# Seven block products in place of eight for the second graph layer, and aggregation columns divided at 250 and 750

## The chip, the cores and the metric

The kernel runs on one core of a Trainium2 chip. The metric is the device time of one execution in microseconds (us); lower is better. An engine is named by what it does: TensorE (PE in the rows; PEld is its weight load, which lies beside the matmuls) multiplies matrices into PSUM, the eight accumulation banks of 128 x 512 fp32; VectorE (DVE), ScalarE (ACT) and GpSimd (POOL) work on elements; SyncE (SP) issues DMAs. Each engine runs its own queue in order, and engines wait for each other by semaphores.

## The reference, cut to what matters

```python
def gnn_layer(x, W, b, src, dst):
    h = x @ W.T + b
    msgs = h[src]
    agg = jax.ops.segment_sum(msgs, dst, num_segments=1250)
    return jax.nn.relu(agg)

xn = _layernorm(x)                         # 1250 x 512
h = gnn_layer(xn, W1, b1, src, dst)        # 20000 edges
g = gnn_layer(h, W2, b2, src, dst)
x = x + g + mix(xn)                        # linear attention and two projections
x = x + ffn(_layernorm(x))                 # eight experts, Sinkhorn gates, top-k routing
```

What this case is about is the second `x @ W.T + b`: a 1250 x 512 matrix times 512 x 512, and the aggregation of the first layer just before it.

## The kernel before

The 1250 rows stand in 10 tiles of TT = 125. The edge list is turned into a matrix AT (AT[source, destination] is the number of edges), so an aggregation is a product with AT. The kernel needs nearly fp32 accuracy from fp32r matmuls, so every operand is kept as two parts, a rounded high part (H) and what is left (L), and each product is three matmuls: high by high, high by low, low by high.

Stages in order of time: layer norm and attention products, the first layer's features `h0` to `h9` (with AT being counted by short bf16 "visits" in between), then the three stages that matter here:

- **First aggregation**, transposed (`sources`, L1031, matmul in L1040): `z{ch}_{f}` for three stretches `ch` of destination columns (CHUNKS, 416, 416 and 418 wide) and four blocks `f` of 128 features, each the sum over 10 source tiles and the two parts H1H and H1L, 20 matmuls. The last 46 visits stand inside the eight units of the first two stretches (`visits`, L762), each before the eleventh matmul of its unit. VectorE writes two small masks for each visit (L1923, L1924) and casts each finished group of counts into AT (L2086).
- ScalarE writes the high part ZH of each z with a Relu (L1536), VectorE the low part ZL (`z_left`, L2076).
- **Second layer's features** (L1085 to L1089): `h2_{i}` for ten tiles, each one PSUM bank, 12 matmuls of 512 columns (four blocks of 128 features, three matmuls each, `terms`, L775), with Z as the stationary side and the weights G2H, G2L as the moving side. The banks turn through 4 to 7. VectorE adds the bias in PSUM (`add_bias`, L1948), ScalarE writes H2H (L1301), VectorE writes H2L (`h2_left`, L2008).
- **Second aggregation** (`collect`, L1138): `o{i}` for ten tiles, 20 matmuls of 512 columns each, over the tiles of H2H and H2L, the tile 9 last (L1157, L1158). VectorE and ScalarE normalise each row block behind it.

GpSimd makes the low part of the second layer's weights, G2L (`split_lo`, L616 to L621), after the last cast of AT, and is idle otherwise from 77 to 300 us. Nothing sets the order of the work but the order in which each engine's code is written. `psum_plan` writes down which unit uses which bank, and `opens(name)` makes TensorE wait until the readers of the bank's last unit are done; `closes(name, ...)` raises the bank's count when the unit is full, and `reads(engine, name)` waits for that count.

Of the kernel before, what the change touches and what calls it, by code (L numbers as in the profile page):

```python
# [52 lines left out]
CHUNKS = [(0, 416), (416, 832), (832, N)]  # L53
# [14 lines left out]
Z_BANKS = ((2, 3, 0, 1), (6, 7, 2, 3), (0, 1, 4, 5))  # L68
LANES = 16
# [18 lines left out]
def psum_plan():  # L88
# [56 lines left out]
    for ch in range(3):  # L145
        for f in range(C):
# [40 lines left out]
def visits_in_products():  # L187
# [17 lines left out]
    spots += [(f"z{ch}_{f}", 10, LATE // 8 + (C * ch + f < LATE % 8)) for ch in range(2) for f in range(C)]  # L205
# [27 lines left out]
def gps_block(nc, x_in, src_t, dst_t, rows_in, win_in, gW1T, gb1, gW2T, gb2, WqT, WkT, WvT, mW1, mW2T,  # L233
# [5 lines left out]
    with ExitStack() as ctx:  # L239
# [18 lines left out]
        def pair(name, shape, off, step=8):  # L258
# [35 lines left out]
        AC = at("AC", [128, 2, N - CHUNKS[2][0]], F32R, 192.75)  # L294

# [35 lines left out]
                  at("LEFT_0c", [128, 1, D], F32R, areas["a"][0] / KB)]  # L331
        HOT_S = small("HOT_S", [128, RING_A, 128], BF16, "a")
# [80 lines left out]
        def view(name, chunks=C):  # L413
# [30 lines left out]
        chunks = [("w2", 0), ("w2", 1), ("w2", 2), ("w1", 2), ("w2", 3), ("w1", 3)] + [(n, c) for n in ("wk", "wq", "wv", "g1", "g2") for c in range(C)]  # L444
        by_dve = [("w1", c) for c in range(C)] + [("wk", 0), ("wk", 3), ("wq", 1), ("wq", 3)] + [(n, c) for n in ("wv", "g1") for c in range(C)]
# [54 lines left out]
        def _(sp):  # L500
# [72 lines left out]
            sp.wait_ge(done["h2_biased"], NT)  # L573
# [22 lines left out]
        def _(pool):  # L596
# [78 lines left out]
            for c in range(C):  # L675
                split_lo("g2", c)
# [63 lines left out]
        def _(pe):  # L740
# [289 lines left out]

            def sources(ch, f, ks, visited=False):  # L1031

                c0, c1 = CHUNKS[ch]
                for k in ks:
                    if ch == 0 and f == 0:
                        pe.wait_ge(done["h1l_ready"], k + 1)
                    for n, h in enumerate((H1H, H1L)):
                        if visited:
                            visits(f"z{ch}_{f}", 2 * k + n)
                        mm = pe.matmul(PS[plan[f"z{ch}_{f}"][0]][:, 0:c1 - c0], h[0:TT, k, 128 * f:128 * (f + 1)], AT[0:TT, k, c0:c1],  # L1040
                                       start=(k == 0 and n == 0), stop=(k == NT - 1 and n == 1))
                if NT - 1 in ks:
                    closes(f"z{ch}_{f}", mm)
# [31 lines left out]
            for f in range(C):  # L1075
                opens(f"z2_{f}")
                sources(2, f, range(NT - 1))
# [4 lines left out]
            for f in range(C):  # L1082
                sources(2, f, (NT - 1,))

            pe.wait_ge(*lo_of("g2", C - 1))  # L1085
            for i in range(NT):
                span = min(ch for ch, (_, c1) in enumerate(CHUNKS) if c1 >= TT * (i + 1))
                pe.wait_ge(done["zl_ready"], (span + 1) * C)
                product(f"h2_{i}", opens(f"h2_{i}")[0:TT, :], (block_of(ZH, i, TT), block_of(ZL, i, TT)), (rows_of(G2H), rows_of(G2L)))  # L1089
# [209 lines left out]
        def _(act):  # L1299
# [232 lines left out]

            for ch, (c0, c1) in enumerate(CHUNKS):
                for f in range(C):
                    reads(act, f"z{ch}_{f}")
                    nc.scalar.activation(ZH[:, f, c0:c1], ps_of(f"z{ch}_{f}")[:, 0:c1 - c0], ACT.Relu).then_inc(done["zh_ready"], 1)  # L1536
            for i in range(NT):
                act.wait_ge(done["h2_biased"], i + 1)
                copy(H2H[0:TT, i, :], ps_of(f"h2_{i}")[0:TT, :]).then_inc(done["h2h_ready"], 1)
# [71 lines left out]
        def _(dve):  # L1611
# [333 lines left out]
            def add_bias(layer, i):  # L1945
                ps = ps_of(f"h{i}" if layer == 1 else f"h2_{i}")[0:TT, :]
# [437 lines left out]
```

## Time and profile before

| | us |
|---|---|
| three runs: median (lowest to highest) | 447.08 (446.76 to 447.33) |
| the profiled execution, own time | 446.48 |
| its span | 444.6 |
| granted TensorE clock, mean | 1.00 of full speed |

One core has one span, so the page is read from its second part on: the busy tenths of each engine in 40 slices, then the chain that ended last, then the groups. A busy TensorE is not a TensorE at its peak, since the ends of pipelined matmuls are modelled: the distance from one start to the next (a chain piece's time over its count) is the cost of a matmul, not the duration in its row.

### The profile page before, as it was taken

To read this page: it belongs to the slowest core of one execution; us is meant where nothing else is said; L and a number is where in the kernel's file an instruction comes from. 1 tells how busy PE (TensorE), PEld (TensorE's weight loads), DVE (VectorE), ACT (ScalarE), POOL (GpSimd) and SP (SyncE) were. 2 spreads that over 40 slices of the span, in tenths; PEclk is the share of its full clock that TensorE was granted. 3 is DMA by queue.
4 is the path that set the end of the run, shared out by engine and by line. 5 is a ranking of instruction groups with operands and counts; after the bars stand their busy time and mean duration, and the time that the engine had idled before them with its cause. 6 is when DMAs were issued, how large, how long until landed. Compare 5 with 4: busy or idle time off the path is not lost.

```text
span 444.6 us, 6723 instructions
## 1 busy us (share of the span) xinstructions
PE 430.9 (97%) x2410; PEld 350.2 (79%) x2410; DVE 314.1 (71%) x977; ACT 154.7 (35%) x284; POOL 74.1 (17%) x108
## 2 busy tenths in 40 slices
PE   8999999999999999999999999999999999888995
PEld 4877788889898988987799998778777766555783
DVE  6989498989887979956777512445546576778972
ACT  3667695214333354412230102221141117541210
POOL 6407823000000000000000040005000000007752
PEclk9999999999999999999999999999999999999999
DMA  8920200180000002012000000007444469107891
GB/s 254 276 88 0 97 0 13 25 217 23 2 1 0 2 0 85 13 24 110 1 3 2 0 1 1 0 1 254 153 133 140 140 188 390 58 1 213 314 365 59
DMA packets 20700, 40.58 MB, mean 91 GB/s; under 512 B 2761, under 2 KB 3097, under 8 KB 20661
## 3 DMA queue, kind: packets, MB, share of 16 engines
q1 hardware_dynamic: 18117, 32.46, 23.3%
q0 software_dynamic: 2544, 7.61, 4.9%
q8 instruction: 23, 0.38, 0.4%
q14 instruction: 16, 0.13, 0.1%
HBM read 30.24 MB, written 10.31 MB: 91 GB/s over the span
## 4 chain that ended last, share of the span: by engine, by line
PE 85%; DVE 9%; ACT 3%; issue 2%; DMA 1%; POOLq 0%; POOL 0%; SPq 0%; DVEq 0%
PE ps L775 34%; PE ps L1040 10%; PE ps L1146 10%; PE ps L965 6%; PE ps L907 6%; PE ps L762 4%; PE ps L983 3%; PE ps L817 2%; ACT scrap_a L1594 2%; PE ps L1163 1%; PE ps L1252 1%; PE ps L918 1%; PE ps L1095 1%; DVE XTL L1678 1%; PE ps L1282 1%
## 5 line engine op out<-in xcount | busy, mean ns | idle before, releaser
L1923 DVE TENSOR_SCALAR RING_D<-places,PLACES 125x170 bf16<-125x170 f16 (+1 forms) x198 | 51.7, 261 | 0.0
L1924 DVE TENSOR_SCALAR RING_S<-iota,HOME 125x128 bf16<-125x128 f16 x198 | 49.1, 248 | 0.0
L1040 PE MATMUL ps<-AT,H1H 125*128 125x416 f32 (+1 forms) x120 | 42.8, 357 | 0.0
L1040 PE MATMUL ps<-AT,H1L 125*128 125x416 f32 (+1 forms) x120 | 42.2, 351 | 0.0
L1146 PE MATMUL ps<-H2H,AT 125*125 125x512 f32 x90 | 36.1, 402 | 0.0
L1146 PE MATMUL ps<-H2L,AT 125*125 125x512 f32 x90 | 35.5, 394 | 0.0
L1163 PE MATMUL ps<-WE0H 128*128 128x512 f32 x129 | 35.5, 408 | 0.0
L620 POOL TENSOR_TENSOR G2L<-RAW_G,G2H 128x512 fp32r<-128x512 f32 x4 | 5.0, 1290 | 179.7 <-DVE AT L2086 179.7
L1948 DVE TENSOR_TENSOR ps<-ps,bias 125x512 f32<-125x512 f32 x20 | 14.0, 699 | 24.8 <-PE ps L775 24.8
L1163 PEld LDWEIGHTS ps<-WE0H 128*128 128x128 f32 x129 | 22.7, 189 | 3.6
L1040 PEld LDWEIGHTS ps<-AT,H1L 125*128 125x128 f32 x120 | 22.6, 189 | 0.3
L762 PEld LDWEIGHTS ps<-RING_D,RING_S 125*125 125x125 bf16 x198 | 19.5, 136 | 4.2
L1040 PEld LDWEIGHTS ps<-AT,H1H 125*128 125x128 f32 x120 | 22.6, 188 | 0.2
L965 PE MATMUL ps<-QTH,CPH 128*128 128x252 f32 x80 | 22.7, 284 | 0.0
L965 PE MATMUL ps<-QTH,CPL 128*128 128x252 f32 x80 | 22.3, 279 | 0.0
L965 PE MATMUL ps<-QTL,CPH 128*128 128x252 f32 x80 | 22.2, 278 | 0.0
L2076 DVE SCALAR_TENSOR_TENSOR ZL<-ps,ZH 128x416 fp32r<-128x416 f32 (+1 forms) x12 | 6.8, 588 | 21.6 <-ACT ZH L1536 21.6
L762 PE MATMUL ps<-RING_D,RING_S 125*125 125x170 bf16 (+1 forms) x198 | 21.3, 237 | 0.0
L1536 ACT ACTIVATE ZH<-ps 128x416 fp32r<-128x416 f32 (+1 forms) x12 | 5.9, 521 | 40.6 <-PE ps L1040 40.6
L1146 PEld LDWEIGHTS ps<-H2H,AT 125*125 125x125 f32 x90 | 16.7, 186 | 4.0 <-issue 0.2
L1146 PEld LDWEIGHTS ps<-H2L,AT 125*125 125x125 f32 x90 | 16.7, 185 | 3.8
L2157 DVE SCALAR_TENSOR_TENSOR X<-ps,X 125x512 f32<-125x512 f32 x9 | 6.2, 691 | 17.2 <-PE ps L1158 17.2
(422 smaller groups left out, 1162.6 us busy)
## 6 DMA issues: line engine op xcount, KB each, us to landing
RAW_E<-in_experts SPq DMA_DIRECT2D x8, 1024.0 KB, 9.5
RAW_AGAIN<-in_experts SPq DMA_DIRECT2D x3, 1024.0 KB
X<-in_x SPq DMA_DIRECT2D x1, 2240.0 KB
out_x<-X SPq DMA_DIRECT2D x10, 224.0 KB
scratch<-X SPq DMA_DIRECT2D x10, 224.0 KB
scratch<-Y SPq DMA_DIRECT2D x10, 224.0 KB
RAW<-in_mW2T SPq DMA_DIRECT2D x4, 256.0 KB, 4.2
RAW_A<-in_mW SPq DMA_DIRECT2D x4, 256.0 KB, 4.6
```

Of the source, the lines that this page charges most:

```text
L762: pe.matmul(PS[4 + g % 2][0:TT, o:o + width(b)], hot_s(v)[:, 0:TT], hot_d(v, width(b)), start=(s == 0), stop=(s == VISITS[b] - 1), skip_gr ...
L775: mm = pe.matmul(ps, stationary[a](c), moving[b](c), start=(first and n == 0), stop=(last and n == len(pairs) - 1))
L817: return pe.matmul(PS[plan[f"mp{f}"][0]][:], w[0][:, c, 128 * f:128 * (f + 1)], w[1][:, c, :], start=first, stop=last)
L907: mm = pe.matmul(ps[:], x[0:TT, i, f], e[0:TT, i % 4, :], start=(i == 0 and n == 0), stop=(i == NT - 1 and n == 2))
L965: mm = pe.matmul(o, w[:, c, block], q[:, c].rearrange("p t n -> p (t n)"), start=False, stop=(c == C - 1 and n == 2), skip_group_check=True)
L983: mm = pe.matmul(ps[:], t[:, c, 128 * f:128 * (f + 1)], v[:, c, :], start=(c == 0 and k == 0), stop=(c == C - 1 and k == 2))
L1040: mm = pe.matmul(PS[plan[f"z{ch}_{f}"][0]][:, 0:c1 - c0], h[0:TT, k, 128 * f:128 * (f + 1)], AT[0:TT, k, c0:c1], start=(k == 0 and n == 0) ...
L1146: pe.matmul(ps, AT[0:TT, k, t], h[0:TT, k, :], start=(k == 0 and n == 0), stop=False)
L1163: pe.matmul(PS[bank][:], WEH[0][:, 0, 0:128], WEH[0][:, 0, :], start=True, stop=True)
L1923: V.tensor_scalar(hot_d(v, width(b)), places[0:ET, 0:width(b)], PLACES[0:ET, v:v + 1], None, ALU.is_equal)
L1924: V.tensor_scalar(hot_s(v), iota[0:ET, :], HOME[0:ET, v:v + 1], None, ALU.is_equal).then_inc(done["marked"], 1)
L1948: V.tensor_tensor(ps, ps, bias[layer - 1][0:TT, :], ALU.add).then_inc(done["h1_biased" if layer == 1 else "h2_biased"], 1)
```

## The change

Two things. The columns of the first aggregation are divided at 250 and 750 (250, 500 and 500 wide), so that each stretch holds whole pairs of 125-row tiles. And the features of the second layer are computed for a pair of tiles at once: Z of a pair is a 2 x 2 matrix of blocks (even and odd tile by lower and upper half of the features, `up` and `down`), the weights are a 2 x 2 matrix of blocks of 256 x 256 (`near` and `far` columns), and the product is made with seven block products, not eight, by Winograd's form of Strassen's scheme. The block sums that this needs are made for the weights once (four sums of 128 x 512 on GpSimd, high parts on ScalarE, low parts on VectorE), and for each pair six sums of 128 x 2 x 125 (the first pair's on VectorE, the others' on GpSimd), four high parts (ScalarE) and four low parts (VectorE). For each pair ScalarE also writes the bias into the bank ahead of the products (`preset`) and copies one block to a second bank (`put_first`); VectorE keeps one block in SBUF (`keep_fifth`) and adds it in two places (`put_fourth`, `put_corner`). The separate addition of the bias is gone.

TensorE's order for a pair p is: `sixth(p)`, `first_and_fifth(p + 1)`, `seventh(p)`, `second_and_third(p)`, `fourth(p)`, where each of the seven products is six matmuls of 256 columns. The even tile gathers in bank 2 or 3 (`h2_{2p}`), the odd one in the "square", bank 6, 7 or 4 in turn, which `first`, `second`, `third` and `h2_{2p+1}` use one after the other.

The core of the diff (allocations, the z parts, the weights' sums and the bodies of the products are left out), in this order: the plan of banks, GpSimd's `combine`, TensorE's order, ScalarE's loop, VectorE's `sums_left` and loop:

```diff
-CHUNKS = [(0, 416), (416, 832), (832, N)]
+CHUNKS = [(0, 250), (250, 750), (750, N)]
+Z_VISITS = [4, 4, 3, 3] + [8] * 4
+LAST_SOURCES = [7, 8, 9, 0, 1, 2, 3, 4, 5, 6]
+SQUARES, EDGES_OUT = (6, 7, 4), (2, 3)
...
-    for i in range(NT):
-        use(f"h2_{i}", high, ("h2h_ready", i + 1), ("h2l_ready", i + 1))
+    for p in range(PAIRS):
+        square, edge_out = SQUARES[p % 3], EDGES_OUT[p % 2]
+        use(f"first{p}", (square,), ("fifth_kept", C + p + 1))
+        use(f"second{p}", (square,), ("fourth_put", NT + p + 1))
+        use(f"third{p}", (square,), ("corner_put", NT + p + 1))
+        use(f"h2_{2 * p}", (edge_out,), ("h2h_ready", 2 * p + 1), ("h2l_ready", 2 * p + 1))
+        use(f"h2_{2 * p + 1}", (square,), ("h2h_ready", 2 * p + 2), ("h2l_ready", 2 * p + 2))
...
+            def combine(p):
+                pool.wait_ge(done["zl_ready"], (span_of(p) + 1) * C)
+                if p == 1:
+                    reads(pool, "rows_freed")
+                else:
+                    reads(pool, f"first{p - 2}")
+                summed(s1, s3, f32(ZH[:, down, o]), ALU.add)
+                summed(s1, s1, f32(ZL[:, down, o]), ALU.add)
+                summed(s3, s2, s3, ALU.subtract)
+                summed(s2, s1, s2, ALU.subtract)
+                if p > 1:
+                    reads(pool, f"h2_{2 * (p - 2)}")
+                summed(s4, f32(ZH[:, down, e]), s2, ALU.subtract)
+                summed(s4, s4, f32(ZL[:, down, e]), ALU.add)
...
+            for n in range(FREED, NT - 1):
+                source(n)
+            first_and_fifth(0)
+            source(NT - 1)
+            for p in range(PAIRS):
+                sixth(p)
+                if p + 1 < PAIRS:
+                    first_and_fifth(p + 1)
+                else:
+                    fourth(p - 1)
+                seventh(p)
+                second_and_third(p)
+                if p != PAIRS - 2:
+                    fourth(p)
...
+            for p in range(PAIRS):
+                round_sums(p + 2, 1)
+                preset(p + 2)
+                round_sums(p + 2, 2)
+                put_first(p + 1)
+                round_sums(p + 2, 3)
+                round_h2(2 * p)
+                round_h2(2 * p + 1)
+                round_sums(p + 2, 4)
...
+            def sums_left(p, j):
+                if p < PAIRS:
+                    if j < 3:
+                        dve.wait_ge(*sum_step(p, 3 + j))
+                    after("s_high", C + 4 * p + j)
+                    hi, lo, whole = sums_of(p, j)
+                    V.tensor_tensor(lo, whole, hi.bitcast(F32), ALU.subtract).then_inc(done["s_low"], 1)
...
+            for p in range(PAIRS):
+                if p:
+                    put_fourth(p)
+                sums_left(p + 2, 1)
+                sums_left(p + 2, 2)
+                if p < PAIRS - 1:
+                    keep_fifth(p + 1)
+                else:
+                    h2_left(2 * p - 1)
+                put_corner(p)
+                sums_left(p + 2, 3)
+                h2_left(2 * p)
+                if p != PAIRS - 2:
+                    h2_left(2 * p + 1)
+                sums_left(p + 2, 4)
```

How the order changes, at three places. On TensorE, in the second layer's features, an excerpt of before: two tiles' products follow each other, each matmul 512 columns wide, and the only waits are for Z.

```order
1733 L775 MATMUL ps<-G2H,ZL 125x512
1734 L775 MATMUL ps<-G2H,ZH 125x512 [waits zl_ready,zh_ready]
1735 L775 MATMUL ps<-G2L,ZH 125x512
1736 L775 MATMUL ps<-G2H,ZL 125x512
1737 L775 MATMUL ps<-G2H,ZH 125x512
```

The changed kernel at the same place, the end of pair 0: the last of `second_and_third(0)` (the six rows on the `sums` tiles), then `fourth(0)`. The name `mix_added` stands for `corner_put`, `qtl_ready` for `fourth_put`, `tl_ready` for `s_low`, `xnl_ready` for `s_sum` (semaphores are used again).

```order
1777 L1197 MATMUL ps<-G2H,sums_4_168 125x256 [waits tl_ready,qtl_ready]
1778 L1197 MATMUL ps<-G2L,sums_4_168 125x256
1779 L1197 MATMUL ps<-G2H,sums_5_169 125x256
1780 L1197 MATMUL ps<-G2H,sums_4_168 125x256
1781 L1197 MATMUL ps<-G2L,sums_4_168 125x256
1782 L1197 MATMUL ps<-G2H,sums_5_169 125x256
1783 L1197 MATMUL ps<-G4H,ZH 125x256 [waits w_lo_dve,mix_added]
1784 L1197 MATMUL ps<-GT,ZH 125x256
```

What moved: a pair's last product now waits for an addition of VectorE (`put_corner`), where a tile's product waited for nothing but Z. On VectorE, before, beside the same products:

```order
1056 L2008 TENSOR_TENSOR H2L<-ps,H2H 125x512 [waits h2h_ready]
1057 L1948 TENSOR_TENSOR ps<-ps,bias_67 125x512 [waits bank_full6]
1058 L2008 TENSOR_TENSOR H2L<-ps,H2H 125x512 [waits h2h_ready]
1059 L1948 TENSOR_TENSOR ps<-ps,bias_67 125x512 [waits bank_full7]
1060 L2008 TENSOR_TENSOR H2L<-ps,H2H 125x512 [waits h2h_ready]
```

and in the changed kernel, in the iteration of pair 0 (`put_corner` is the row of L2426, and the two rows of L2399 ahead of it are `sums_left(2, 1)` and `sums_left(2, 2)`):

```order
1085 L2399 TENSOR_TENSOR sums_1_165<-raw_sums_1_176,sums_0_164 128x2x125 [waits th_ready,xnl_ready]
1086 L2399 TENSOR_TENSOR ZL<-ZLF,sums_2_166 128x2x125 [waits th_ready,xnl_ready]
1087 L2415 COPY H2F<-ps 125x256 [waits cph_ready]
1088 L2426 TENSOR_TENSOR ps<-ps,H2F 125x256 [waits bank_full6]
1089 L2399 TENSOR_TENSOR ZH<-ZHF,sums_3_167 128x2x125 [waits th_ready]
1090 L2265 TENSOR_TENSOR H2L<-ps,H2H 125x512 [waits h2h_ready] x2
```

What moved: the low parts of the sums of the pair after next stand ahead of this pair's `put_corner`. On GpSimd, before, there is the making of G2L and then the preparation for the gates:

```order
54 L620 TENSOR_TENSOR G2L<-RAW_G_96,G2H 128x512 [waits w_hi,adj_hi]
55 L620 TENSOR_TENSOR G2L<-RAW_G_96,G2H 128x512 [waits w_hi] x3
56 L679 MEMSET gw_182 128x128 [waits bank_full7]
```

and in the changed kernel, the six sums of pair 2 (`combine(2)`), of which the fifth waits for bank 2, that is for `h2_0`:

```order
66 L743 TENSOR_TENSOR raw_sums_1_176<-ZHF,ZH 128x2x125 [waits bank_full6,zl_ready,xnl_ready]
67 L743 TENSOR_TENSOR raw_sums_1_176<-raw_sums_1_176,ZL 128x2x125 [waits xnl_ready]
68 L743 TENSOR_TENSOR ZHF<-ZLF,ZHF 128x2x125 [waits xnl_ready]
69 L743 TENSOR_TENSOR ZLF<-raw_sums_1_176,ZLF 128x2x125 [waits xnl_ready]
70 L743 TENSOR_TENSOR raw_sums_5_177<-ZH,ZLF 128x2x125 [waits bank_full2,xnl_ready]
71 L743 TENSOR_TENSOR raw_sums_5_177<-raw_sums_5_177,ZL 128x2x125 [waits xnl_ready]
```

What moved: 28 additions that did not exist (four for the weights, six for each of four pairs) stand between G2L and the memset, each waiting for the one before it.

## Rows read from the trace of the kernel before

**Rows 1.** The page: engines' busy time, then the chain that ended last, by engine.

```profile
PE 430.9 (97%) x2410; PEld 350.2 (79%) x2410; DVE 314.1 (71%) x977; ACT 154.7 (35%) x284; POOL 74.1 (17%) x108
...
PE 85%; DVE 9%; ACT 3%; issue 2%; DMA 1%; POOLq 0%; POOL 0%; SPq 0%; DVEq 0%
```

**Rows 2.** The chain that ended last, in order of time: start us, us, what.

```profile
144.28 2.78 PE ps L965 x24
...
147.51 2.83 PE ps L965 x24
...
223.25 1.88 PE ps L1040 x10
...
229.97 3.81 PE ps L1040 x20
...
246.58 0.45 PE ps L762 x6
...
255.04 0.32 PE ps L762 x5
255.37 17.18 PE ps L1040 x90
272.55 27.90 PE ps L775 x120
300.45 4.21 PE ps L1146 x18
...
320.87 0.12 PE ps L1120 x2
```

**Rows 3.** One line's instructions, L965: durations min/median/max, first and last start, form.

```profile
L965 PEld LDWEIGHTS ps<-QTL,CPH x80: 187/188/192, 104.2 to 186.5; 128*128 128x128 f32 x80
```

**Rows 4.** Groups by form: x count, busy us, mean ns of one, idle before.

```profile
L620 POOL TENSOR_TENSOR G2L<-RAW_G,G2H 128x512 fp32r<-128x512 f32 x4 | 5.0, 1290 | 179.7 <-DVE AT L2086 179.7
L2008 DVE TENSOR_TENSOR H2L<-ps,H2H 125x512 fp32r<-125x512 f32 x10 | 6.8, 682 | 0.1
L2086 DVE CAST AT<-ps 125x260 fp32r<-125x260 f32 x1 | 0.4, 419 | 0.0
L1818 DVE TENSOR_TENSOR edge<-edge 111x250 f32<-111x250 f32 x1 | 0.4, 420 | 0.0
L1301 ACT ACTIVATE H2H<-ps 125x512 fp32r<-125x512 f32 x10 | 6.0, 598 | 22.6 <-DVE ps L1948 22.6
```

**Rows 5.** Timeline, 300 to 303 us, end of the second layer: start, us, engine, what.

```profile
300.05 0.39 PE L775 MATMUL ps<-G2H,ZL 128*125 128x512 f32 x1
300.29 0.40 PE L1146 MATMUL ps<-H2H,AT 125*125 125x512 f32 x1
300.49 0.70 DVE L1948 TENSOR_TENSOR ps<-ps,bias 125x512 f32<-125x512 f32 x1 [1.52 <-PE ps L775]
300.51 0.21 POOL L679 MEMSET gw<- 128x128 f32 x1 [39.21 <-PE ps L775]
...
300.80 0.20 POOL L680 TENSOR_TENSOR fold<-ident 128x8 f32<-128x8 f32 x1
```

**Rows 6.** Timeline, 219 to 222 and 361 to 363 us: back-to-back VectorE, and a wait of TensorE.

```profile
220.74 0.69 DVE L1948 TENSOR_TENSOR ps<-ps,bias 125x512 f32<-125x512 f32 x1
221.34 0.68 DVE L2004 TENSOR_TENSOR H1L<-ps,H1H 125x512 fp32r<-125x512 f32 x1
...
361.55 0.29 DVE L2195 TENSOR_REDUCE s<-P 125x8 f32<-125x80 f32 x1
361.90 0.29 PEld L1193 LDWEIGHTS ps<-s,onesr 125*125 125x125 f32 x2 [0.65 <-DVE s L2195]
```

**Rows 7.** Timeline, 43 to 49 us: GpSimd and VectorE both reading SBUF, then the undisturbed group.

```profile
43.22 2.99 POOL L626 TENSOR_TENSOR XNL<-XF,XNH 125x512 fp32r<-125x512 f32 x2 [0.70 <-ACT XNH L1301]
...
44.04 1.02 DVE L1685 TENSOR_TENSOR WQL<-RAW_A,WQH 128x512 fp32r<-128x512 f32 x1
...
L1685 DVE TENSOR_TENSOR WVL<-RAW_A,WVH 128x512 fp32r<-128x512 f32 x4 | 2.7, 680 | 0.0
```

**Rows 8.** Busy time of engines by stretch: us, PE PEld DVE ACT POOL, PEclk, DMA share.

```profile
272.55:300.45 27.90, 27.90 (x121) 22.24 (x121) 12.56 (x21) 6.05 (x11) 0.00 (x0) 1.00 0.00 1
...
380.00:393.00 13.00, 10.19 (x55) 6.71 (x54) 9.26 (x36) 7.83 (x15) 0.00 (x0) 1.00 0.01 2
```

More of the change, by code:

```diff
@@ new lines, in sixfold, with square, edge_out, parts @@
+            def sixfold(ps, a, b):
+                for c in range(2):
+                    for m, n in ((0, 0), (0, 1), (1, 0)):
+                        mm = pe.matmul(ps, a[m][:, c, :], b[n][:, c, :], start=False, stop=(c == 1 and m == 1), skip_group_check=True)
+                return mm
+            def square(p, w):
+                return PS[plan[f"first{p}"][0]][0:TT, w]
+            def edge_out(p, w):
+                return PS[plan[f"h2_{2 * p}"][0]][0:TT, w]
+            def parts(rows, cols):
+                return ZH[:, rows, cols], ZL[:, rows, cols]
@@ L1078, in _, with fourth @@
+            def fourth(p):
+                opens(f"h2_{2 * p + 1}")
+                closes(f"h2_{2 * p + 1}", sixfold(square(p, near), parts(down, odd[p]), mixed_with(p, 4)))
+            source(0)
             with pe.If(large[0] > 0):
@@ L1081, in _ @@
                 pe.nop()
[L1082 to L1089, printed above, removed]
+            for n in range(1, FREED - 1):
+                source(n)
+            closes("rows_freed", source(FREED - 1))
+            for n in range(FREED, NT - 1):
+                source(n)
+            first_and_fifth(0)
[10 more added lines that the diff above has]
+                    fourth(p)
             def turn_y(i):
@@ L1531, in _, with tiles_in @@
                 split_hi("g2", c)
-            for ch, (c0, c1) in enumerate(CHUNKS):
-                for f in range(C):
[L1535 to L1539, printed above, removed]
+            def tiles_in(t, n):
+                return t.rearrange("p (q t n) -> p q t n", t=2, n=TT)[:, :, n, :]
@@ new lines, in square, with keep_fifth, put_fourth @@
+            def square(p, w):
+                return ps_of(f"first{p}")[0:TT, w]
+            def keep_fifth(p):
+                if p < PAIRS:
+                    after("first_put", C + p + 1)
+                    V.tensor_copy(fifth_of(p), square(p, far)).then_inc(done["fifth_kept"], 1)
+            def put_fourth(p):
+                reads(dve, f"second{p}")
+                after("fifth_kept", C + p + 1)
+                V.tensor_tensor(ps_of(f"h2_{2 * p}")[0:TT, far], square(p, near), fifth_of(p), ALU.add).then_inc(done["fourth_put"], 1)
@@ new lines, in put_corner @@
+            def put_corner(p):
+                reads(dve, f"third{p}")
+                V.tensor_tensor(square(p, far), square(p, near), fifth_of(p), ALU.add).then_inc(done["corner_put"], 1)
+            combine_first()
+            for j in (1, 2, 3, 4):
+                sums_left(0, j)
+            weights_left(1, 1)
+            weights_left(3, 3)
+            weights_left(2, 4)
+            sums_left(1, 1)
+            sums_left(1, 2)
+            keep_fifth(0)
+            sums_left(1, 3)
```

227 lines of the change are left out of this document (203 added, 24 removed).

## The prediction

> **What bounds the kernel now.** I read the page's engine line and the shares of the chain first: TensorE is busy 97% of the span and carries 85% of the chain that ended last [rows 1]. Then the chain in order of time around the change: from 223.25 to beyond 304 us every piece of it is TensorE, with nothing in between [rows 2]. So in this stretch a matmul saved is time saved, and a wait of TensorE is time lost, one to one. The other engines have room there: in the 27.90 us of the second layer VectorE is busy 12.56 us, ScalarE 6.05 and GpSimd not at all [rows 8]. What a matmul costs is the chain's time over its count: 27.90 / 120 = 0.2325 us at 512 columns, 3.81 / 20 = 0.1905 at 416, (2.78 + 2.83) / 48 = 0.1169 at 252 [rows 2]. The line through the first and last gives 0.1160 at 250, 0.1187 at 256, 0.2272 at 500 (and 0.1899 at 416, so it holds).
>
> **The work on TensorE.** Second layer: 120 matmuls x 0.2325 = 27.90 become 5 pairs x 7 x 6 = 210 matmuls x 0.1187 = 24.93: **-2.97**. An eighth of the products is gone, but a narrow matmul costs a little over half of a wide one. Aggregation: 240 x 0.1905 = 45.72 become 80 x 0.1160 + 160 x 0.2272 = 45.63: -0.09. The 46 visits stay 46, at 0.45 / 6 = 0.075 [rows 2]. Five matmuls of one row are added that mark the rest of a bank; the nearest row is a small matmul, 0.12 / 2 = 0.06 [rows 2]: +0.30. Together **-2.8**, if nothing waits.
>
> **The waits.** I laid the four queues out in the order of the changed code, each instruction with its duration by a row. GpSimd: 1.290 us for 512 elements and 0.20 for 8 [rows 4, 5], on a line 0.72 for 250. VectorE: 0.420 for 250 from SBUF and 0.419 for 260 from PSUM, 0.682 for 512 [rows 4]; back to back the next one starts 0.09 before the end (220.74 + 0.69 against 221.34 [rows 6]), so 0.33 each for the narrow ones in a row. ScalarE 0.598 for 512 [rows 4]. From the place where the next matmul could start to a reader's start: 300.29 to 300.49, 0.20 [rows 5]. VectorE's end to TensorE's start: 361.84 to 361.90, 0.06 [rows 6]. The same layout of the kernel before ends `o0` at the same 304.9 as the trace.
>
> The loop that I find is this. `fourth(p)` accumulates on what `put_corner(p)` wrote. On VectorE `put_corner(p)` stands behind `sums_left(p + 2, 2)`, which waits for the fifth sum of `combine(p + 2)` on GpSimd, and GpSimd makes that sum only when `h2_{2p}` is full. But `h2_{2p}` is full at the end of `second_and_third(p)`, the piece directly ahead of `fourth(p)`. So TensorE has nothing to do while its own result goes round: 0.20 to GpSimd (rows say 0.22), sum 0.72, hand over 0.04, then on VectorE 0.33 (`sums_left`), 0.33 (`keep_fifth`), 0.42 (`put_corner`), and 0.06 back: **2.1 us** (2.15 in the layout). It happens for p = 0, 1, 2; for p = 3 there is no pair 5 to sum, and pair 3's fourth product stands later. 3 x 2.15 = **+6.45**. Bounds for one loop: GpSimd's sum has no row at this shape; in proportion to 1.290 it would be 0.63, and 1.29 if a 128 x 2 x 125 cost as much as a full one; so 2.05 to 2.7. I take 0.72, by the line between the two rows [rows 4, 5].
>
> Smaller waits. `sixth(p)` and `seventh(p)` use the same half of a bank, with `put_fourth(p)` between, covered by `first_and_fifth(p + 1)` (12 x 0.1187 = 1.42) against 0.20 + up to 0.9 of queue + 0.42 + 0.06: 0.1 to 0.2 for p = 1 to 3, and 0.5 for p = 4, where only `fourth(3)` (0.71) covers it. Sum **+1.0** (0 to 1.5). `o0` takes bank 2, which `h2_8` has just filled: 0.20 + 0.60 + 0.04 + 0.68 + 0.06 = 1.58, less 0.71 of `fourth(4)`: **+0.9**; before, the bank was long free. Each of some 8 wake-ups shows its first weight load, about 0.1 (the nearest row: a start for which load and matmul are both waited [rows 6]; 0 to 0.19, the load's duration [rows 3]): **+0.8** (0 to 1.5).
>
> What is hidden: the 46 masks and casts of VectorE, the four G2L and weight sums on GpSimd (from about 253 to 269) and the first pair's sums on VectorE end near 271, while TensorE needs the first of them at 271.5 (`first_and_fifth(0)`, second half) and the sixth product's at 274.1; that cover is thin, and a sum that came 3 us later would cost what it is late.
>
> Sum: -2.8 + 6.45 + 1.0 + 0.9 + 0.8 = **+6.35**. Made against the profiled execution (446.48, span 444.6) it gives 452.8; that execution lies 0.6 under the median of the runs, so I put it on the median: 447.08 + 6.35 = **453.4 us**. Nothing after `o0` is touched but shifted.
>
> **A rule weighed.** A VectorE subtraction with both inputs in SBUF took 1.02 us while GpSimd was in an addition, against 0.680 alone, and that pair of GpSimd additions took 2.99 against 2 x 1.29 [rows 4, 7]: each waited for the other to finish. I have this in the layout; without it the first pair's sums would be ready near 263, and the total 0.2 less. The Trainium skill, "SBUF — State Buffer", section "Who interferes with whom", says that such an instruction and a GpSimd one that reads SBUF lock each other out for a whole instruction, whichever starts first; the rows agree. By that rule the order of two starts decides.
>
> **The rivals.**
> (a) *GpSimd wins the race.* When the fifth sum ends, GpSimd's sixth and VectorE's `sums_left` both want to read. My layout lets VectorE start first, by 0.04 us. If GpSimd does, VectorE stands 0.6 longer in each loop: 3 x 0.6 and a little elsewhere, +2.0, 455.4 us. For it: the gap is tiny. Against: GpSimd's own next start takes 0.08 (300.72 to 300.80 [rows 5]). The same direction has a sum slower than 0.72: 0.85 gives 455 to 456, and at 1.29 six sums a pair (7.7 us and more) would outlast the pair itself, some 13 us more.
> (b) *The loop is shorter or is covered*, so that the narrow instructions cost half of what I took (stall 1.0): 450.
> (c) *The other side: faster.* If TensorE's waits were all hidden, so that GpSimd's sum was already made when `second_and_third(p)` ended, the result would be -2.8 + 0.9 = 445.2. It decides at a loop of 0.3 us; that needs the fifth sum not to wait for `h2_{2p}`, and the order of the changed kernel shows that wait (row 70 of its GpSimd queue). Only a reading error of mine would bring it.
> (d) *Weight loads bound the narrow matmuls.* The load's row says 0.187 [rows 3]; if they could not overlap, 210 x (0.187 - 0.119) = +14 on top, 468. Against it: the same loads stand under matmuls 0.1169 apart [rows 2, 3].
> (e) *The clock falls.* In the loop TensorE pauses 2.1 in 7.5 us. The granted clock is 1.00 in every stretch, also from 380 to 393 us, where TensorE is busy 10.19 of 13.00 in short bursts [rows 8]. If it fell to 1.2 of 2.4 GHz for half of the 25 us of products, +12, 465.
> (f) *The change doesn't do what it says* in that VectorE or GpSimd falls behind before the first pair: +1 to +3, 455 to 456, with (a).
>
> **How the numbers follow.** Forecast 453.4, with its own range 452 to 454.8: 0.50. (a) with (f): 0.27. (b): 0.10. (c): 0.06. (d): 0.02. (e): 0.05. Up to 457.3 on the upper side and down to 450.8 on the lower leaves out about 2 in 10: (c), (d), (e) and the ends of (a) and (b). 0.2% is 0.9 us, about what a measurement can tell from no change; faster by more 0.06, within 0.02, slower 0.92.
>
> **What the profile after would show.** Right: the chain's second-layer stretch goes through GpSimd and VectorE three times; TensorE idle some 2.1 us before the matmuls with G4H as moving side, three times and not a fourth, released by VectorE; GpSimd's fifth sums start 0.2 behind a matmul; matmuls of 256 columns 0.119 apart; `o0` starts at about 306.6 in place of 300.3. Wrong: no idle time there (c), idle of 2.8 (a), narrow matmuls 0.187 apart (d), a granted clock under 1.00 (e).

## The result, and the profile after

| | us |
|---|---|
| before, five runs beside the changed kernel: median (lowest to highest) | 447.08 (446.76 to 447.59) |
| changed kernel, five runs: median (lowest to highest) | 456.14 (455.92 to 457.73) |
| ratio, with its 95% interval | 1.0213 (1.0201 to 1.0226) |
| profiled execution after: own time, span | 456.14, 454.4 |

The change makes the kernel slower by 9.1 us, 2.1%. The range (450.8 to 457.3) holds the time; the forecast's own range (452 to 454.8) doesn't, since 2.7 us more were lost than the sum had. The page of the changed kernel, which answers to [rows 1]:

```profile
PE 433.6 (95%) x2505; PEld 349.7 (77%) x2505; DVE 333.0 (73%) x1018; ACT 168.2 (37%) x324; POOL 97.2 (21%) x137
...
PE 81%; DVE 10%; ACT 3%; issue 2%; DMA 1%; POOL 1%; SPq 0%; POOLq 0%; DVEq 0%
```

TensorE has 95 matmuls more and a smaller share of the chain, and GpSimd, which had 0% of it, has 1%. The chain in order of time, to be held beside [rows 2] (L1140 and L1185 are the aggregation, L1129 the five small matmuls, L1197 the block products, L1333 the second aggregation; L2399 is `sums_left`, L2415 `keep_fifth`, L2426 `put_corner`, L2421 `put_fourth`, L1488 ScalarE's copies):

```profile
223.93 1.17 PE ps L1140 x10
...
237.75 2.53 PE ps L1140 x11
240.28 0.11 PE ps L1129
240.39 2.24 PE ps L1140 x9
...
273.13 1.42 PE ps L1197 x12
274.56 1.83 PE ps L1185 x8
276.38 4.36 PE ps L1197 x36
...
280.88 0.64 POOL raw_sums L743
...
282.30 0.35 DVE ps L2426
...
282.69 3.08 PE ps L1197 x24
```

Before, nothing stood between two pieces of TensorE here. Now the chain leaves it three times, for GpSimd's fifth sum and three instructions of VectorE. The same place in the timeline (start, us, engine, what, idle time before it and its releaser):

```profile
280.45 0.28 PE L1197 MATMUL ps<-G2H,sums 128*125 128x256 f32 x1
280.77 0.60 ACT L1488 ACTIVATE H2H<-ps 125x512 fp32r<-125x512 f32 x1 [0.29 <-PE ps L1197]
280.88 0.63 POOL L743 TENSOR_TENSOR raw_sums<-ZH,ZLF 128x250 f32<-128x250 f32 x1 [2.90 <-PE ps L1197]
281.54 0.42 DVE L2399 TENSOR_TENSOR ZL<-ZLF,sums 128x250 fp32r<-128x250 f32 x1 [1.17 <-POOL raw_sums L743]
281.59 0.90 POOL L743 TENSOR_TENSOR raw_sums<-raw_sums,ZL 128x250 f32<-128x250 f32 x1
281.88 0.42 DVE L2415 COPY H2F<-ps 125x256 f32<-125x256 f32 x1
282.21 0.42 DVE L2426 TENSOR_TENSOR ps<-ps,H2F 125x256 f32<-125x256 f32 x1
...
282.69 0.39 PE L1197 MATMUL ps<-G4H,ZH 128*125 128x256 f32 x1 [1.96 <-DVE ps L2426]
...
282.91 0.29 PE L1197 MATMUL ps<-GT,ZH 128*125 128x256 f32 x1
```

The row of the matmul ahead ends at 280.73, and the next one starts at 282.69: a pause of 1.95 to 1.96. The same pause stands at 288.17 and at 295.61, and not for the fourth and fifth pair: 5.85 us of idle time in all. What it costs is read from start to start: 280.45 to 282.69 is 2.24 where 0.12 is usual, so 2.12 us are lost, three times, 6.36 us. The matmul behind the pause takes 0.22 to the next start (282.69 to 282.91), 0.10 more than usual. Two smaller waits behind them, for `put_fourth(4)` and for bank 2:

```profile
306.09 0.18 PEld L1197 LDWEIGHTS ps<-G3H,sums 128*125 128x125 f32 x1 [0.54 <-DVE ps L2421]
...
309.91 0.18 PEld L1333 LDWEIGHTS ps<-H2H,AT 125*125 125x125 f32 x1 [0.94 <-ACT H2H L1488]
```

What the prediction had at nearly nothing was the clock. The same stretch in windows of one microsecond (us, TensorE's busy time and instructions, granted clock, DMA):

```profile
299.00:300.00 1.00, 1.00 (x8) 0.57 0.00 0
300.00:301.00 1.00, 1.00 (x7) 0.50 0.00 0
301.00:302.00 1.00, 1.00 (x6) 0.50 0.00 0
302.00:303.00 1.00, 1.00 (x9) 0.73 0.00 0
```

What is missing to full speed in these windows is 0.43 + 0.50 + 0.50 + 0.27 = 1.70 us, so for 3.4 us, from 299.1 to 302.5, TensorE runs at 1.2 GHz instead of 2.4. Its cost is a little less, and is again read from the starts:

```profile
299.49 0.41 PE L1197 MATMUL ps<-G2H,ZL 128*125 128x256 f32 x1
299.70 0.41 PE L1197 MATMUL ps<-G2H,ZH 128*125 128x256 f32 x1
```

Some sixteen matmuls start 0.213 apart in place of 0.118, which is 1.5 us. And the small matmuls of the aggregation cost more than their piece of the chain says:

```profile
234.42 0.39 PE L1140 MATMUL ps<-AT,H1H 125*128 125x500 f32 x1
234.74 0.09 PEld L1129 LDWEIGHTS ps<-zero 1*128 1x128 bf16 x1 [0.24 <-issue]
234.74 0.18 PE L1129 MATMUL ps<-zero 1*128 1x12 bf16 x1
234.85 0.49 PE L1140 MATMUL ps<-AT,H1L 125*128 125x500 f32 x1
235.18 0.39 PE L1140 MATMUL ps<-AT,H1H 125*128 125x500 f32 x1
235.41 0.39 PE L1140 MATMUL ps<-AT,H1L 125*128 125x500 f32 x1
```

From 234.42 to 235.18 two wide matmuls and the small one took 0.76; two wide ones take 0.46 (235.18 to 235.41 is 0.23). So the small one costs 0.30, not 0.11, and not the 0.06 that I took.

Where the 9.8 us between the two spans (444.6 and 454.4) lie: the aggregation took 273.13 - 223.93 + 1.83 = 51.03 in place of 49.30, **+1.7**; the second layer's features 309.94 - 273.13 - 1.83 = 34.98 in place of 27.90, **+7.1**; 0.7 belongs to a late start, which is there from 14 us on and which executions of every kernel here show now and then; 0.3 is left behind `o0`.

### The profile page after: what moved, and what is told of

It reads as the page before. It is cut to its first block, busy times and chain, and to the rows that moved or that the text cites. A ratio compares the mean times of both kernels' runs of the same rounds, so it can differ in the third digit from the quotient of the medians.

```text
span 454.4 us, 7083 instructions
## 1 busy us (share of the span) xinstructions
PE 433.6 (95%) x2505; PEld 349.7 (77%) x2505; DVE 333.0 (73%) x1018; ACT 168.2 (37%) x324; POOL 97.2 (21%) x137
## 4 chain that ended last, share of the span: by engine, by line
PE 81%; DVE 10%; ACT 3%; issue 2%; DMA 1%; POOL 1%; SPq 0%; POOLq 0%; DVEq 0%
PE ps L871 27%; PE ps L1333 9%; PE ps L1140 6%; PE ps L1061 6%; PE ps L1003 6%; PE ps L1197 6%; PE ps L1185 4%; PE ps L858 4%; PE ps L1079 3%; ACT scrap_a L1851 2%; DMA RAW_A<-in_mW 1%; PE ps L1350 1%; PE ps L1439 1%; PE ps L1014 1%; DVE stat L1906 1%
## 5 line engine op out<-in xcount | busy, mean ns | idle before, releaser
L735 POOL TENSOR_TENSOR G2L<-RAW_G,G2H 128x256 fp32r<-128x256 f32 (+1 forms) x4 | 3.9, 1013 | 177.8 <-DVE AT L2349 177.8
L1333 PE MATMUL ps<-H2H,AT 125*125 125x512 f32 x90 | 36.3, 403 | 0.8 <-ACT H2H L1488 0.8
L1333 PE MATMUL ps<-H2L,AT 125*125 125x512 f32 x90 | 35.5, 395 | 0.0
L1140 PE MATMUL ps<-AT,H1H 125*128 125x250 f32 (+1 forms) x80 | 25.7, 342 | 0.0
L1140 PE MATMUL ps<-AT,H1L 125*128 125x250 f32 (+1 forms) x80 | 25.5, 339 | 0.0
L807 POOL DMA_INDIRECT YX<-scratch,idx_half x2 | 2.9, 1446 | 92.4 <-DVE idx L2624 92.1
L1333 PEld LDWEIGHTS ps<-H2H,AT 125*125 125x125 f32 x90 | 16.7, 186 | 5.0 <-ACT H2H L1488 0.9
L1333 PEld LDWEIGHTS ps<-H2L,AT 125*125 125x125 f32 x90 | 16.7, 186 | 3.9
L1833 ACT ACTIVATE rstd<-mv,eps 125x1 f32<-125x1 f32 x10 | 3.0, 296 | 39.8 <-DVE mv L2505 39.8
L871 PE MATMUL ps<-MPH,SH 128*125 128x512 f32 x40 | 16.9, 422 | 0.0
L871 PE MATMUL ps<-WKH,XTH 128*125 128x512 f32 x40 | 16.5, 413 | 0.3 <-DVE XTL L1935 0.2
L871 PE MATMUL ps<-WQH,XTH 128*125 128x512 f32 x40 | 16.6, 416 | 0.0
```

Source lines behind the costliest of these rows:

```text
L871: mm = pe.matmul(ps, stationary[a](c), moving[b](c), start=(first and n == 0), stop=(last and n == len(pairs) - 1))
L1333: pe.matmul(ps, AT[0:TT, k, t], h[0:TT, k, :], start=(k == 0 and n == 0), stop=False)
```

## The experiments

All ratios are to the kernel before, run beside each. Some executions are 2 to 3 us longer than the others, whatever the kernel (the kernel before: 446.05 to 449.67 us beside the reordered queues). Two such executions were profiled, of the reordered queues and of the exchanged banks, and they are late from the start: ScalarE's first XTH stands at 16.75 and 16.60 us, where it stands at 14.43 in the kernel before. So what is under 1 us is read from stretches of the trace.

### One line moved: the loop

```diff
                 sums_left(p + 2, 1)
-                sums_left(p + 2, 2)
                 if p < PAIRS - 1:
                     keep_fifth(p + 1)
...
                 put_corner(p)
+                sums_left(p + 2, 2)
                 sums_left(p + 2, 3)
```

> The changed kernel with one line of VectorE's loop moved: sums_left(p + 2, 2), which waits for GpSimd's fifth sum, stands behind put_corner(p) in place of ahead of keep_fifth(p + 1). Theory L (the loop): the three waits of TensorE ahead of fourth(0), fourth(1), fourth(2), 1.95 us each in the trace of the changed kernel, disappear, since nothing else that put_corner(p) needs is late: keep_fifth 0.34 and put_corner 0.35 to 0.42 fit into the 1.42 us of second_and_third(p). With them goes the fall of the granted clock behind the third wait (about 1.6 us), if it comes from the pauses. 456.1 - 5.85 - 1.6 = 448.7 us (448.2 to 449.5). Rival R1: put_corner is late in any case, because VectorE and ScalarE have too much between two pairs: a wait of 0.5 to 1.5 us stays in each pair, 450.5 to 454. Rival R2: the clock falls without the pauses, from the narrow matmuls: 450.3 with the clock at half behind the third pair.

Measured: 451.38 us (451.04 to 452.90), ratio 1.0102 (1.0080 to 1.0123), 4.8 us under the changed kernel. The granted clock stayed at 1.00 until the last matmul. The timeline behind the first pair:

```profile
280.91 0.38 PE L1197 MATMUL ps<-G4H,ZH 128*125 128x256 f32 x1 [0.37 <-DVE ps L2426]
...
281.40 0.91 POOL L743 TENSOR_TENSOR raw_sums<-raw_sums,ZL 128x250 f32<-128x250 f32 x1
...
281.69 0.89 DVE L2399 TENSOR_TENSOR ZH<-ZHF,sums 128x250 fp32r<-128x250 f32 x1
...
282.50 1.27 DVE L2265 TENSOR_TENSOR H2L<-ps,H2H 125x512 fp32r<-125x512 f32 x2
...
284.12 0.42 DVE L2421 TENSOR_TENSOR ps<-ps,H2F 125x256 f32<-125x256 f32 x1
...
284.59 0.39 PE L1197 MATMUL ps<-G3H,sums 128*125 128x256 f32 x1 [0.61 <-DVE ps L2421]
```

The wait for `put_corner` is 0.37 in place of 1.96. But the work that stood ahead of it now stands ahead of `put_fourth(1)`, and `seventh(1)` waits: 0.61 here and 0.80 in the next pair, 2.4 us of idle time in four such waits, where the changed kernel had 0.3 in one. The loop was real; I had taken for granted that nothing would take its place. The time lies in R1's range, though at another product than R1 had named.

### The loop cut at another point: a place of its own for the fifth sum

```diff
+        raw_late = [at(f"raw_late{n}", [128, 2, 128], F32, 56 + n) for n in range(3)]
...
-            s, raw = sums[p % 2], raw_sums[p % 2]
+            s, raw = sums[p % 2], raw_sums[p % 2] if p < 2 else {1: raw_sums[p % 2][1], 5: raw_late[p - 2]}
...
-                if p > 1:
-                    reads(pool, f"h2_{2 * (p - 2)}")
```

> The changed kernel with a place of its own for the fifth sum of pairs 2, 3 and 4 (three rows of H2L that are not in use until the last tiles), so that GpSimd needs not wait for h2_{2p}; VectorE's, ScalarE's and TensorE's orders are those of the changed kernel. It breaks the same loop at another point than the moved line did. Theory L: the waits of 1.95 us ahead of fourth(1) and fourth(2) go altogether, since all six sums of combine(p + 2) are done before h2_{2p} is full; ahead of fourth(0) up to 1.8 us may stay, because VectorE's queue is full there (z_left, the weights' low part) and GpSimd's third sum of pair 3 and VectorE's low parts hold each other up. With the small waits of before: 456.1 - 5.2 - 1.6 (clock) = 449.3 us (448.7 to 450.5), lower than the moved line's 451.4, since put_fourth is no longer behind GpSimd's sums. Rival: GpSimd's wait for h2_{2p} is not what holds put_corner, but VectorE's own work: no more than 1 us of each loop comes back, 453 to 455.

Measured: 450.39 us (449.85 to 453.25), ratio 1.0107 (1.0080 to 1.0133), inside what was expected.

```profile
279.45 0.94 DVE L2398 TENSOR_TENSOR sums<-raw_sums,sums 128x250 fp32r<-128x250 f32 x1
...
280.31 0.88 DVE L2398 TENSOR_TENSOR ZL<-ZLF,sums 128x250 fp32r<-128x250 f32 x1
...
281.92 0.38 PE L1196 MATMUL ps<-G4H,ZH 128*125 128x256 f32 x1 [1.72 <-DVE ps L2425]
```

The first pair's wait is 1.72 in place of 1.96, and it is another one: nothing of GpSimd stands in the chain, and VectorE comes late out of its own work (two low parts of 0.94 and 0.88 that take 0.42 when GpSimd is quiet). For pairs 1 and 2 TensorE doesn't wait for `put_corner` at all; `put_fourth(2)` costs 0.6 instead. So GpSimd's wait for `h2_{2p}` and VectorE's order together made the loop, as the prediction said: taking away either one opens it.

### The pauses filled: what the clock costs

```diff
             def fourth(p):
+                if p < PAIRS - 2:
+                    pe.wait_ge(done["zh_ready"], 2 * C + 1)
+                    pe.wait_ge(done["zl_ready"], 2 * C + 1)
+                    for n in range(12):
+                        pe.matmul(PS[0][0:TT, near], ZH[:, 0, even[0]], G2H[:, 0, near], ...)
                 opens(f"h2_{2 * p + 1}")
```

> The changed kernel with twelve more matmuls of 256 columns (12 x 0.119 = 1.43 us) on TensorE ahead of fourth(0), fourth(1) and fourth(2), written into a bank that nobody reads. They stand in the pause and change no result. The loop is not broken: TensorE still waits 1.95 - 1.43 = 0.5 us there. Theory P (pauses): the granted clock falls in the changed kernel at 299 to 303 us (0.50 to 0.73) because TensorE had paused three times in 22 us; with the pauses filled it stays 1.00 and the 16 slow matmuls (0.213 us apart in place of 0.119) cost nothing more: 456.1 - 1.6 = 454.5 us (454.2 to 455). Rival: the clock falls from the load itself (weight loads and narrow matmuls) or by chance: it falls here too, and the time is 456.0 to 456.5.

Measured: 455.04 us (454.50 to 455.32), ratio 1.0175 (1.0154 to 1.0196). Thirty-six matmuls more, and 1.1 us less. The first filled pause, and a window of those in which the clock had fallen:

```profile
280.31 1.60 PE L1256 MATMUL ps<-G2H,ZH 128*125 128x256 f32 x12
282.43 0.38 PE L1197 MATMUL ps<-G4H,ZH 128*125 128x256 f32 x1 [0.52 <-DVE ps L2431]
```

```profile
300.00:302.00 2.00, 2.00 (x17) 1.00 0.00 0
```

The chain still goes three times through GpSimd and VectorE, with the same durations; only TensorE is not idle meanwhile, and its clock stays at 2.4 GHz. That separates the two costs of the loop: the wait itself, and the clock behind it. The time is 0.5 above what was expected. Counted from start to start, the stretch of the features gives back 1.3 us (35.14 to 33.84): the fall's 1.5, less 0.2 for a wait for `put_fourth(3)` that the changed kernel does not have, since its clock is low just there and VectorE is done in time.

### Only the third pause filled

The same edit with `if p == 2`.

> The changed kernel with the twelve filling matmuls of 1.43 us ahead of fourth(2) only: TensorE pauses 1.95, 1.95 and 0.5 us, not 1.95 three times (the granted clock fell after the third) and not 0.5 three times (it stayed 1.00). Theory S: the fall needs the sum of the pauses over a stretch longer than one pair, so that with the third filled the clock stays 1.00: 456.1 - 1.6 = 454.5 us (454.2 to 455). Rival: two pauses are enough to lower the clock, and it falls somewhere from 290 us on: 456.0 to 457, since the filler adds nothing.

Measured: 455.44 us (454.72 to 456.12). Theory S falls. In the profiled execution the clock fell behind the *first* pause, at 283.0 us, and was back at 1.00 before the second:

```profile
283.00:284.00 1.00, 1.00 (x7) 0.50 0.00 0
```

Of its six executions four had a mean granted clock of 0.995 or 0.996 (455.27, 455.60, 455.80 and 456.12 us) and two 0.999 and 1.000 (454.72 and 454.92). A fall alone takes 1.70 / 455 = 0.004 from the mean, so these are four executions with one fall and two with none. So it is not a sum of three pauses, and not the same in every execution.

### The changed kernel again

> The changed kernel once more, beside the other on the same chip. Expected 456.1 us (455.9 to 457.3), with three waits of 1.95 us and, by the reading that each of them can start a fall of the granted clock of some 3.3 us, one or two falls in an execution, not always at the same one of the three. Rival: the fall belongs to the third pause; then it stands there again.

Measured: 457.03 us (454.76 to 457.53), ratio 1.0223 (1.0202 to 1.0243). In the profiled execution the clock fell twice, behind the first and behind the third pause:

```profile
282.00:284.00 2.00, 1.99 (x9) 0.52 0.00 0
...
300.00:302.00 2.00, 2.00 (x11) 0.50 0.00 0
```

The five executions: mean clock 1.000 with 454.76 us, 0.995 with 457.17, and 0.990 with 456.76, 457.03 and 457.53. One fall of 3.4 us at half speed takes 1.70 / 455 = 0.0037 from the mean, and the end of the program up to 0.002, so 0.995 is one fall and 0.990 two. The one execution without a fall is 1.4 us under the first median of this kernel. By the same count its first five executions had one fall each (0.994 to 0.996) but for one, which had two (0.990, 457.73 us).

Over all runs: in the kernels with three pauses of 1.95 us (the changed one, run twice, the one without the small matmuls and the one with the even banks exchanged) 18 of 21 executions had a mean clock of 0.996 or less; with two such pauses it was 4 of 6, with the one of 1.72 us 1 of 6. In the runs without them or with the pauses cut to 0.5 us (one line moved, all pauses filled, the columns alone, the queues reordered, all together) it was none of 47. Why one pause of 1.95 us is followed by a fall and the next is not, no run here shows.

### The columns alone

In the kernel before, `CHUNKS = [(0, 250), (250, 750), (750, N)]` and the visits 4, 4, 3, 3, 8, 8, 8, 8; nothing else.

> The kernel before with only the columns of the first aggregation divided at 250 and 750, and the visits spread 4, 4, 3, 3, 8, 8, 8, 8; the second layer's features are those of before. Theory: the division itself costs 80 x 0.1183 + 160 x 0.2290 = 46.10 against 45.72, +0.4 us: 447.1 to 447.8. Rival: the 1.7 us by which the aggregation grew in the changed kernel (49.3 to 51.0) belong to the division, because VectorE's masks and casts come too late for the visits when the first stretch is short: 448.5 to 449.

Measured: 446.96 us (446.52 to 447.73), ratio 1.0000 (0.9989 to 1.0012). Its aggregation lasts 273.29 - 223.83 = 49.46 us against 49.30 [rows 2]. The division of the columns is free, and the 1.7 us are not its doing.

```profile
273.29 27.92 PE ps L776 x120
```

### The five small matmuls taken away

```diff
-                            unmark(f"z1_{f}", c1 - c0)
...
-                        mm = pe.matmul(PS[...][:, 0:c1 - c0], h[0:TT, k, ...], AT[0:TT, k, c0:c1], ...)
+                        s = shifted(f"z{ch}_{f}") if k == 0 and n == 0 else 0
+                        mm = pe.matmul(z_of(ch, f, s), h[0:TT, k, ...], AT[0:TT, k, c0 - s:c1], ...)
```

`z_of` gives columns 12 to 512 of the bank in those units, and the first matmul begins 12 columns further to the left.

> The changed kernel without the five small matmuls (12 columns, one row) that mark the rest of a bank. In their place the first matmul of those five units is 512 columns wide and begins 12 columns to the left, over the whole bank, and the unit stands at columns 12 to 512 of its bank. Theory M: a small matmul costs far more than the 0.11 us of its own piece of the chain, since the next weight load cannot lie under it: from the matmul ahead to the second behind it is 0.76 us (234.42 to 235.18) against 2 x 0.229, so 0.30 each; 5 x 0.30 = 1.5 us go: 454.6 us (454.3 to 455.0). Rival: they cost 0.06 to 0.11 each and the rest is a matter of the records: 455.6 to 455.9.

Measured: 454.57 us (454.15 to 455.70), ratio 1.0174 (1.0151 to 1.0197). A unit of 500 columns is one piece again, 4.58 where it was 2.53 + 0.11 + 2.24 = 4.88:

```profile
242.14 4.58 PE ps L1148 x20
```

The whole aggregation lasts 271.15 - 223.46 + 1.83 = 49.52, and with it 1.5 us are gone, 0.30 for each of the five, as the starts had said.

### The even banks exchanged

`SQUARES, EDGES_OUT = (6, 7, 4), (3, 2)` in place of `(2, 3)`.

> The changed kernel with the two even banks in the other order (3, 2) and nothing else: h2_8 is gathered in bank 3, and o0 begins in bank 2, which h2_6 filled a pair earlier. Theory: the wait of o0 for the high and low part of h2_8, 0.75 us in its row and 0.9 from the last product's place, goes: 455.2 us (454.9 to 455.6). Rival: o0 waits instead for o1's turn or for H2L of h2_7, which VectorE writes late: 455.8 to 456.2.

Measured: 454.58 us (453.29 to 456.90), ratio 1.0159 (1.0126 to 1.0192). The spread is too wide to settle 0.9 us by the times. The chain settles the mechanism: 24 products and then `o0`, with nothing between, where the changed kernel had an ACT piece and a wait of 0.75.

```profile
307.82 3.10 PE ps L1197 x24
310.91 4.33 PE ps L1333 x18
```

In this execution the clock fell behind the second pause, which ends at 291.89, and only there:

```profile
293.00:294.00 1.00, 1.00 (x7) 0.56 0.06 16
294.00:295.00 1.00, 1.00 (x7) 0.50 0.00 0
```

### Both queues reordered, and everything together

```diff
                 if p:
                     put_fourth(p)
-                sums_left(p + 2, 1)
-                sums_left(p + 2, 2)
-                if p < PAIRS - 1:
-                    keep_fifth(p + 1)
-                else:
-                    h2_left(2 * p - 1)
+                    sums_left(p + 1, 3)
+                    h2_left(2 * p - 1 if p < PAIRS - 1 else 2 * p - 2)
+                    sums_left(p + 1, 4)
+                keep_fifth(p + 1)
                 put_corner(p)
-                sums_left(p + 2, 3)
-                h2_left(2 * p)
-                if p != PAIRS - 2:
-                    h2_left(2 * p + 1)
-                sums_left(p + 2, 4)
+                if p == PAIRS - 1:
+                    h2_left(2 * p - 1)
+                sums_left(p + 2, 1)
+                if p != PAIRS - 2:
+                    h2_left(2 * p)
+                sums_left(p + 2, 2)
+            h2_left(NT - 1)
...
                 preset(p + 2)
-                round_sums(p + 2, 2)
                 put_first(p + 1)
+                round_sums(p + 2, 2)
```

> The changed kernel with VectorE's whole loop in another order and one step of ScalarE's moved, arithmetic and TensorE as they are. VectorE: keep_fifth(p + 1) and put_corner(p) come ahead of every sums_left of pair p + 2, and of the low parts that are left, two or three stand behind put_fourth(p), the others behind put_corner(p). ScalarE: put_first(p + 1) ahead of round_sums(p + 2, 2). In the run with one line moved the 5.8 us of the loops came back by 3.5: 2.7 to 2.8 us went instead into waits for put_fourth(1 to 3), 0.6, 0.8 and 0.8 (VectorE then did sums_left(3), two H2L and sums_left(4), some 3 us in a row, between put_corner and put_fourth), and for put_corner, 0.37, 0.17 and as much again. Theory Q (the queues' order alone): laid out with the durations of that run the new order leaves waits of 0.2 to 0.6 us in all, and o0's 0.9: 456.1 - 7.2 (loops and small waits) - 1.6 (clock) = 447.3 us (446.5 to 448.3). Rival: VectorE has too much work between two pairs (4.6 of 5.0 us) in any order: 449.5 to 451.5.

Measured: 447.96 us (447.32 to 451.27), ratio 1.0022 (1.0002 to 1.0041), inside what was expected. From start to start the features take 27.0 us in place of 35.14; what is left of waits is 0.2, 0.2 and 0.4 for `put_corner` and the 0.9 of `o0`. With the mark and the banks of the last two experiments added:

> As the kernel with both queues reordered, and also without the five small matmuls (first matmul of five units 512 wide, which took 1.5 us off), and with the two even banks in the other order (3, 2), so that h2_8 is in bank 3 and o0 begins in bank 2, which h2_6 left free earlier. Theory: 447.3 - 1.5 - 0.9 = 444.9 us (444.0 to 446.0), under the kernel before (446.9) by 0.2 to 0.6%: what is left of seven products in place of eight when nothing waits is the 2.97 us of matmuls less some small waits. Rival: the gains overlap (o0 has to wait for the high or low part of h2_6 or h2_7 in place of the bank): 445.8 to 447.

Measured: 445.49 us (444.66 to 447.63), ratio 0.9965 (0.9947 to 0.9984): the seven products do win over eight, by 0.35%. The chain through the features:

```profile
274.60 4.35 PE ps L1202 x36
...
299.29 4.33 PE ps L1338 x18
```

and all that TensorE's weight loads and matmuls waited for between 270 and 312 us (total, times, longest):

```profile
PEld ps L1202 <- DVE ps L2431: 1.0, 3, 0.5
...
PE ps L1202 <- DVE ps L2431: 0.2, 1, 0.2
```

The features last 1.42 + (299.29 - 274.60) = 26.11 us against 27.90, of which 24.8 are the 210 matmuls, 0.118 each, and 1.3 the waits that are left; the aggregation, from its first matmul to the first block product and with the eight matmuls behind that, takes 49.80 us against 49.30, so it gives 0.5 back. 1.8 - 0.5 = 1.3 us in these two stretches; the medians differ by 1.7.

## Why the prediction was right, and what it missed

| term | predicted | measured | read from |
|---|---|---|---|
| features, 120 to 210 matmuls | -2.97 | -3.1 | starts 0.118 apart, 210 x 0.118 = 24.8 |
| three loops | +6.45 | +6.36 | start to start, 3 x 2.12 |
| `put_fourth` | +1.0 | +0.8 | 0.17, 0.15, 0 and 0.50 for pairs 1 to 4 |
| `o0` and bank 2 | +0.9 | +0.92 | start to start; gone with the banks exchanged |
| wake-ups | +0.8 | +0.7 | six starts 0.22 from the next, not 0.12; `o0` 0.30, not 0.23 |
| the five small matmuls | +0.30 | +1.5 | taken away |
| columns at 250 and 750 | -0.09 | +0.16 | columns alone |
| the granted clock | 0 (rival, 0.05) | +1.5 a fall, one or two falls | starts in the windows |

The measured sizes are distances between starts in the profiled execution, less the usual distance. They add up: the features take 35.14 us from the first block product to `o0`, without the eight matmuls of the aggregation between (the chain has 34.98, since the piece ahead of it ends 0.16 behind the first start), against 27.90 before.

**What bounds.** Right: in this stretch every wait of TensorE was lost one to one, and the pieces of the chain over their counts gave the narrow matmul: 1.42 / 12 = 0.118 for 256 columns (0.1187 expected), 1.17 / 10 = 0.117 for 250 (0.1160).

**The loop.** Right in place, number and members, three times and not a fourth, and in size: 2.12 for 2.15. In that size two misses cancel, which is luck. GpSimd's sum of 250 elements took 0.62 to 0.63 and not the 0.72 of my line through 512 and 8 elements [rows 4, 5]; in proportion to 1.290 it is 0.63, the lower bound, and the line's foot was an addition of 8 elements, far from the size asked for. But GpSimd started 0.31 behind the place where the next matmul could have stood (280.57 to 280.88), not 0.20 to 0.22. The row for that step [rows 5] is one of VectorE; ScalarE, which waits for the same bank, starts at 280.77, 0.11 ahead of GpSimd, and much the same in the other two loops.

**The race (a).** VectorE started first in all three loops (281.54 against 281.59), as the layout had it, and the rival came to nothing. The rows after show both directions: a low part of VectorE that starts ahead of GpSimd takes 0.42 and GpSimd's sum 0.90 in place of 0.63; one that starts behind takes 0.89 (281.69 in the run with one line moved). The Trainium skill, "SBUF — State Buffer", section "Who interferes with whom", says that the one that starts first holds the other off for a whole instruction; these rows agree.

**The small matmuls.** Wrong by a factor of five. The step that failed is "the nearest row is a small matmul, 0.12 / 2 = 0.06". That row was a pair of like matmuls in a row of their own. Here a matmul of 12 columns stands between wide ones: its own weight load comes only 0.32 after the wide one's start (234.42 to 234.74), and under its 0.11 the next weight load of 0.19 cannot lie, so the next two starts are 0.33 apart where 0.23 is usual. What a matmul costs is not in its own piece, but in the distance between its neighbours.

**The clock (e).** Wrong in chance and in size. I looked for pauses in the kernel before and found TensorE busy 10.19 of 13.00 us with the clock at 1.00 [rows 8], and took it that pauses of 2.1 us would do no more; but no pause in that kernel's trace is longer than 1.2 us. The runs show that the longer ones do more: a fall to 1.2 GHz lasts 3.4 us and costs 1.5 us, and comes once or twice in most executions, behind any of the three pauses. With pauses of 0.5 us in the same places no execution of five had a mean clock under 0.997. My rival had half of 25 us at the low clock, 12 us; a fall is an eighth of that.

**Rivals (b), (c), (d), (f).** Nothing was hidden; the weight loads lay under the narrow matmuls, which are 0.119 apart; and the first pair's sums were ready in time, with less than 0.1 us lost before 280.45. (c) was false of this kernel. It said that without the loop the result would be 445.2, and the kernel with everything together runs at 445.49, but that is not (c) come true: this kernel has neither the small matmuls nor the wait of `o0`, both of which (c) kept, and it has 1.3 us of waits, which (c) had not.

**The sum.** 453.4 + 1.2 (small matmuls) + 0.25 (columns) - 0.1 (products) - 0.1 (loops) - 0.2 (`put_fourth`) - 0.1 (wake-ups) + 1.5 (one fall) = 455.9, and 456.14 was measured. The two terms that the sum had at 0.3 and at nothing, 2.7 us together, are the whole miss. The range held them only because its upper side had been left for (a) and (f), neither of which happened; to that extent the hit is luck.

## What to carry to other kernels

When an algorithm saves an eighth of the products but makes each one depend on a neighbour engine, lay out every queue and look for a path from a unit's own end back to its next unit: the path's length is lost in each round, and it is opened by the order of one queue or by one buffer more. After opening it look again, since the work that moved stands ahead of the next thing that is waited for; here one moved line gave back 4.8 of 9.1 us and the whole order 8.2, the clock's share with it. And price a tiny matmul between wide ones by the distance of its neighbours, and a repeated pause of about 2 us on TensorE by more than itself.

## What the hardware showed that I had not expected

- TensorE's granted clock fell from 2.4 to 1.2 GHz for 3.4 us after a pause of 1.95 us, in places that differ from one execution to the next, and it stayed at 1.00 in the profiled execution in which the same pauses were cut to 0.5 us by matmuls that nobody reads. With the low clock a matmul of 256 columns started every 0.213 us in place of 0.118.
- Of two engines that wait for the same bank, ScalarE started 0.04 us behind the end of the last matmul's row and GpSimd 0.15.
- A bf16 matmul of 12 columns and one row cost 0.30 us between fp32r matmuls of 500 columns; a wide matmul that covers the same columns cost nothing that can be measured.
- A GpSimd addition of 128 x 250 took 0.63 us alone and up to 1.01 beside VectorE's instructions; VectorE's low part of the same size 0.41 alone and 0.88 to 0.94 behind GpSimd's start.
